# Grouped attention in smaller units: one pair of heads and 512 queries at a time, in a two-block transformer kernel

## The chip, the core and the metric

The kernel runs on one core of one Trainium2 chip. The metric is the time of the whole program on the device in microseconds (us), from its first to its last instruction with what little lies around them. Before the change the median of 3 runs is 2143.96 us (2143.17 to 2151.37).

Five engines work beside each other, each with a queue of its own that it takes strictly in order: TensorE (PE: matmuls, and PEld for loading the weights of one), VectorE (DVE), ScalarE (ACT), GpSimd (POOL) and SyncE (SP, which here only starts transfers). They meet at semaphores alone: an instruction may wait until a semaphore has reached a number, and may raise one when it ends.

## The reference

The program is two blocks with an attention and a feed-forward part each. The change touches one of the four parts only, the attention with grouped heads ahead of the first mixture of experts, over T = 2048 tokens of width 128:

```
N_HEADS = 16;  N_KV = 4;  NUM_REP = 4;  HEAD_DIM = 8
q = (x @ qw + qb).reshape(B, S, N_HEADS, HEAD_DIM).transpose(0, 2, 1, 3)
k = (x @ kw + kb).reshape(B, S, N_KV, HEAD_DIM).transpose(0, 2, 1, 3)      # v alike
k = jnp.repeat(k, NUM_REP, axis=1)
scores = jnp.einsum('bhqd,bhkd->bhqk', q, k) / np.sqrt(HEAD_DIM).astype(np.float32)
attn = jax.nn.softmax(scores, axis=-1)
out = jnp.einsum('bhqk,bhkd->bhqd', attn, v)
out = out.transpose(0, 2, 1, 3).reshape(B, S, D)
return out @ ow + ob
```

Four query heads share each of the four key heads. Every head has 2048 x 2048 scores, and all of them are made, exponentiated, and multiplied by the values.

## The kernel before

The attention is cut into NU = 16 units. A unit is one key head (with its four query heads, two pairs of two) and 512 queries (one of NC = 4 chunks). For every unit the kernel does two things.

**Maxima.** The softmax subtracts each row's maximum. To have it, the scores are made once in the layout of queries by keys (`pe_job`, L847: two matmuls of a pair of heads, 128 queries by 512 keys each, into two banks of PSUM), and VectorE reduces both banks at once (`v_job`, L865, 128x1024). There are UM = 32 such jobs in a unit. After the last of them VectorE folds the partial maxima (MM, L871), GpSimd negates them and splits them in three bf16 parts (`g_neg`), TensorE turns them into rows (job "rows", L850), VectorE copies these out (NMP, L875), and SP writes them by 12 small transfers into three extra rows of the queries' operand QST (`sp_gqa_rows`, L907), so that the next kind of matmul subtracts the maximum by itself.

**Scores, exponentials, values.** For each of the 16 tiles of 128 keys (kt) and each of the two pairs (jj) there is a step, 32 in a unit. I call the step's number i = 2 kt + jj. TensorE makes the scores of the pair again, now keys by queries (`pe_gqa`, L942: two matmuls of 512 columns into two of the three banks 0 to 2, which go round). ScalarE takes the exponential of each bank (`act_gqa`, L986) and writes it to the probability buffer PB (a part of `tmpb`), which holds two key tiles of four heads. TensorE then multiplies values by probabilities (`pe_values`, L920), in half queries: step i multiplies the half jj of the key tile before for all four heads, four matmuls on 32 columns of the array each, accumulating in bank 3. After the unit's last key tile both halves are still due and follow in one go.

**The end of a unit.** ScalarE copies bank 3 to PV (`act_values`, L974) after the first key tile of the next unit, TensorE turns PV (job "values", L854, in step i = 3 of the next unit), and VectorE divides by the sums (L881 a reciprocal, L883 a multiplication).

The order of the work is written out by hand. `ahead(u, i)` says which jobs TensorE and VectorE do in step i of unit u: always one maximum job, EARLY = 12 steps ahead of where it belongs; "rows" four steps after the last maximum of a unit; "values" in step 3. `first_jobs` lists what is done ahead of the first step: the 32 maxima of unit 0, three of unit 1, rows of unit 0, and nine more of unit 1, 44 maxima in all. Jobs take turns on two sets of two banks (4 and 5, 6 and 7), so TensorE can begin job n when VectorE has finished job n-2 (`s_mfree`).

The waits that matter, each with its semaphore: a step's score matmuls wait for the first of the two exponentials of the step before (`s_exp`, since three banks go round); an exponential waits for its scores (`s_qk`), the first one of a key tile also for the values of two key tiles before (`s_pv`, since PB holds two); the values of a key tile wait for its last exponential (`s_exp`), those of a new unit also for the copy of bank 3 (`s_pvc`). The first step waits for the rows (`s_row`) and for the stacked queries and keys (`s_stack_rest`: transfers through `scr_q` and `scr_k`, started by `sp_stacks` and `act_stacks`).

Of the kernel before, what the change touches and what calls it, by code (L numbers as in the profile page):

```python
# [16 lines left out]
F32 = mybir.dt.float32  # L17
# [6 lines left out]
P = 128  # L24
T = 2048
# [32 lines left out]
def build(nc, A, out):  # L58

    ctx = ExitStack()  # L60
    with ctx:
# [62 lines left out]
        def cs(c):  # L124
            return slice(CH * c, CH * c + CH)
# [548 lines left out]
        PAIRS = H0 // 2  # L674
        NU = NKV * NC
        QST = sb("QST", [P, PAIRS, T], BF16, b0)
        KST = sb("KST", [P, NKV, T], BF16, b0)
# [7 lines left out]
        MX = sb("MX", [P, 2, 2, TPC, NC], F32, b0)  # L685
        MM = sb("MM", [P, 2 * 2 * TPC], F32, b0)
        NG = sb("NG", [P, 2 * 2 * TPC], F32, b0)
        NB3 = sb("NB3", [P, 3, 2 * 2 * TPC], BF16, b0)
        NMP = sb("NMP", [3 * 2 * 2 * TPC, 2, P], BF16, b0)
        identb = sb("identb", [P, P], BF16, b0)  # L690
        RD = sb("RD", [P, TPC, REP], F32, b0)
        scr_q = nc.dram_tensor("scr_q", (3, P, T), BF16).ap()
# [11 lines left out]
        s_const2 = sem("s_const2")  # L704
        UI = NT * REP
        UM = UI // 2
        EARLY, LATE = 12, 3

        def ahead(u, i):

            jobs = []
            if i == 3 and u:
                jobs.append(("values", u - 1))
            v, m = u + 1 + (i + EARLY) // UM, (i + EARLY) % UM
            if v < NU:
                jobs.append(("max", v, m))
            if i + EARLY == UM + LATE and u + 1 < NU:
                jobs.append(("rows", u + 1))
            return jobs

        first_jobs = [("max", 0, m) for m in range(UM)] + [("max", 1, m) for m in range(LATE)] + [("rows", 0)] + \
                     [("max", 1, m) for m in range(LATE, EARLY)]
        job_at = {job: n for n, job in enumerate(first_jobs + [j for u in range(NU) for i in range(UM) for j in ahead(u, i)]
                                                 + [("values", NU - 1)])}

# [108 lines left out]
        def pe_job(pe, job):  # L834
            n, what, u = job_at[job], job[0], job[1]
            b = mbank(n)
            if what == "rows":
                pe.wait_ge(s_neg, u + 1)
            if what == "values":
                pe.wait_ge(s_pvc, u + 1)  # L840
            if n >= 2:
                pe.wait_ge(s_mfree, n - 1)
            if what == "max":
                g, qc, (jj, t, kc) = u // NC, u % NC, (job[2] // (TPC * NC), job[2] // NC % TPC, job[2] % NC)
                for x in range(2):
                    r = slice(64 * x, 64 * x + SK)
                    pe.matmul(PS[:, b + x, :], QST[r, 2 * g + jj, CH * qc + P * t:CH * qc + P * t + P], KST[r, g, cs(kc)],  # L847
                              start=True, stop=True).then_inc(s_mjob, 1)
            elif what == "rows":
                pe.matmul(PS[0:3 * 2 * 2 * TPC, b, 0:P], NB3[:, :, :].rearrange("p a m -> p (a m)"), identb[:, :],  # L850
                          start=True, stop=True).then_inc(s_mjob, 2)
            else:
                for t in range(TPC):
                    m = pe.transpose(PS[:, b, P * t:P * t + P], PV[:, P * t:P * t + P], ident[:, :])  # L854
                m.then_inc(s_mjob, 2)

        def v_job(v, chain, job):
# [3 lines left out]
            if what == "max":  # L861
                m = job[2]
                if m == 0 and u:
                    v.wait_ge(s_mm, u)
                r = v.tensor_reduce(MX[:, :, m // (TPC * NC), m // NC % TPC, m % NC], PS[:, b:b + 2, :], AX.X, ALU.max)  # L865
                if m < UM - 1:
                    r.then_inc(s_mfree, 1)
                else:
                    chain.link(r)
                    v.sem_inc(s_mfree, 1)  # L870
                    v.tensor_reduce(MM[:, :], MX[:, :, :, :, :].rearrange("p x j t k -> p (x j t) k"), AX.X, ALU.max).then_inc(s_mm, 1)  # L871
            elif what == "rows":
                if u >= 2:
                    v.wait_ge(s_row[u % 2], ROWS * (u // 2))
                v.tensor_copy(NMP[:, u % 2, :], PS[0:3 * 2 * 2 * TPC, b, 0:P]).then_inc(s_nmp, 1)  # L875
                v.wait_ge(s_nmp, u + 1)
                v.sem_inc(s_mfree, 1)
            else:
                g, qc = u // NC, u % NC
                b7 = PS[:, b, :].rearrange("p (t j c) -> p t j c", t=TPC, j=REP)  # L880
                chain.link(v.reciprocal(RD[:, :, :], b7[:, :, :, HD]))  # L881
                ao = AO[:, TPC * qc:TPC * qc + TPC, 32 * g:32 * g + 32].rearrange("p t (j c) -> p t j c", j=REP)
                v.tensor_tensor(ao, b7[:, :, :, 0:HD], RD[:, :, :].unsqueeze(3).to_broadcast([P, TPC, REP, HD]), ALU.mult).then_inc(s_ao, 1)  # L883
# [15 lines left out]
        def sp_gqa_rows(sp):  # L899
            for u in range(NU):  # L900
                g, qc = u // NC, u % NC
                sp.wait_ge(s_nmp, u + 1)
                for a in range(3):
                    for x in range(2):
                        for jj in range(2):
                            at = 2 * 2 * TPC * a + 2 * TPC * x + TPC * jj
                            sp.dma_start(QST[64 * x + SK + a:64 * x + SK + a + 1, 2 * g + jj, cs(qc)].rearrange("r (t p) -> r t p", p=P),  # L907
                                         NMP[at:at + TPC, u % 2, :]).then_inc(s_row[u % 2], 16)

        ROWS = 3 * 2 * 2 * 16  # L910

        def pe_values(pe, u, kt, half):

            if half == 0:
                if kt == 0 and u:
                    pe.wait_ge(s_pvc, u)
                pe.wait_ge(s_exp, u * UI + (kt + 1) * REP)
            h = slice(CH // 2 * half, CH // 2 * (half + 1))
            for j in range(REP):
                last = pe.matmul(PS[32 * j:32 * j + 32, 3, h], VS[:, kt, u // NC, :], PB[:, kt % 2, j, h],  # L920
                                 start=(kt == 0 and half == 0), stop=(kt == NT - 1 and half == 1),
                                 tile_position=(0, 32 * j), skip_group_check=True)
            if half:
                last.then_inc(s_pv, 1)

        def pe_gqa(pe):
# [4 lines left out]
            pe.wait_ge(s_stack_rest, STACKED)  # L931
            for u in range(NU):
                g, qc = u // NC, u % NC
                pe.wait_ge(s_row[u % 2], ROWS * (u // 2 + 1))
                for i in range(UM):
                    kt, jj = i // 2, i % 2
                    at = UI * u + 2 * i
                    if at >= 2:
                        pe.wait_ge(s_exp, at - 1)
                    for x in range(2):  # L940
                        r = slice(64 * x, 64 * x + SR)
                        pe.matmul(PS[:, (at + x) % 3, :], KST[r, g, P * kt:P * kt + P], QST[r, 2 * g + jj, cs(qc)],  # L942
                                  start=True, stop=True).then_inc(s_qk, 1)
                    for job in ahead(u, i):
# [24 lines left out]
        def act_values(a, u):  # L969

            a.wait_ge(s_pv, NT * (u + 1))
            if u:
# [3 lines left out]
        def act_gqa(a):  # L976
            for u in range(NU):
                for kt in range(NT):
                    if kt == 1 and u:
                        act_values(a, u - 1)  # L980
                    if NT * u + kt >= 2:
                        a.wait_ge(s_pv, NT * u + kt - 1)
                    for j in range(REP):
                        at = UI * u + REP * kt + j
                        a.wait_ge(s_qk, at + 1)
                        a.activation(PB[:, kt % 2, j, :], PS[:, at % 3, :], ACT.Exp, scale=HD ** -0.5).then_inc(s_exp, 1)  # L986
            act_values(a, NU - 1)
# [4 lines left out]
        def v_gqa(v, chain):  # L992
            for job in first_jobs:
                v_job(v, chain, job)
            for u in range(NU):
                for i in range(UM):
                    for job in ahead(u, i):
                        v_job(v, chain, job)
# [1013 lines left out]
```

## Time and profile before

| | us |
|---|---|
| median of 3 runs | 2143.96 |
| the profiled execution | 2147.42 |
| its span, first to last instruction | 2145.6 |
| reductions for maxima, VectorE, L865 x512 | 585.3 busy, 1217 ns each |
| exponentials, ScalarE, L986 x1024 | 554.0 busy, 595 ns each |
| values, TensorE, L920 x4096 | 326.4 busy, 393 ns each |
| scores for the exponentials, TensorE, L942 x1024 | 201.4 busy, 390 ns each |
| scores for the maxima, TensorE, L847 x1024 | 206.6 busy, 401 ns each |
| VectorE, share of the whole span | 64% |
| TensorE, share of the whole span | 80% |

Consecutive instructions overlap inside an engine, so a busy time is not a rate: what one instruction costs in a row of equals is the distance of their starts. In the rows further down, an entry with "xN" is N instructions merged, its duration reaches from the first one's start to the last one's end, and an idle time in brackets stands in front of an entry where the engine had nothing to do, with the one that ended it. A matmul in fp32 is shown as two instructions. The first score matmul for an exponential starts at 466.14 us, the last values are multiplied at 1107.16 us; that stretch is what the change is about.

### The profile page before, as it was taken

Reading aid. Unit: us, or ns where it says so; the run is one execution under the profiler, and the core shown is the slowest. Engines: PE = TensorE matmul, PEld = TensorE weight load, DVE = VectorE, ACT = ScalarE, POOL = GpSimd, SP = SyncE. Lnnn points to the kernel's source line nnn. Section 1 sums busy time; section 2 is a strip of 40 time slices with the busy share of each in tenths; the row PEclk is TensorE's granted clock in tenths of the full one; section 3 lists DMA queues with packets and bytes.
Section 4 is the critical chain, followed back from the end, with each engine's and each line's share of the span. In section 5 each row is a group of like instructions: output and inputs, shape, how many; then the busy total and the mean of one; then the engine's idle time right before and its main releaser. Section 6 shows DMA issues by size and latency. Waiting matters only on the chain.

```text
span 2145.6 us, 27944 instructions
## 1 busy us (share of the span) xinstructions
PE 1723.7 (80%) x10324; PEld 786.0 (37%) x10324; DVE 1363.8 (64%) x2683; ACT 1163.1 (54%) x2116; POOL 267.3 (12%) x336
## 2 busy tenths in 40 slices
PE   3599237269999999999875994989899988489998
PEld 2599225012222222222223442444444444334443
DVE  3898775599999999999622335556656656322222
ACT  3465103028888888888862336556666655212222
POOL 1265003000000000000000002111111111111110
PEclk7899658559999999999996996999999999699999
DMA  1000000430000000000012420000000000122320
GB/s 40 1 1 1 0 0 8 93 47 2 2 2 2 2 2 2 2 2 2 17 26 41 84 63 1 4 12 16 15 15 15 15 0 1 30 43 47 59 51 29
DMA packets 76094, 42.58 MB, mean 20 GB/s; under 512 B 21920, under 2 KB 72224, under 8 KB 75840
## 3 DMA queue, kind: packets, MB, share of 16 engines
q1 hardware_dynamic: 74576, 37.90, 8.6%
q10 hardware_dynamic: 1392, 3.02, 0.7%
q8 instruction: 77, 1.26, 0.3%
q14 instruction: 49, 0.40, 0.1%
HBM read 37.55 MB, written 3.15 MB: 19 GB/s over the span
## 4 chain that ended last, share of the span: by engine, by line
PE 52%; DVE 30%; ACT 7%; DMA 4%; issue 4%; POOL 1%; SPq 0%; ACTq 0%; DVEq 0%; POOLq 0%
DVE MX L865 17%; PE PS L1347 6%; PE PS L920 5%; PE PS L1353 5%; PE PS L1779 4%; PE PS L1780 4%; PE PS L1789 4%; PE PS L942 3%; DMA SB<-scr_w 3%; PE PS L433 3%; PE PS L1298 3%; ACT tmpb L986 3%; PE PS L1317 2%; PE PS L1189 2%; DVE MS L534 2%
## 5 line engine op out<-in xcount | busy, mean ns | idle before, releaser
L986 ACT ACTIVATE tmpb<-PS 128x512 f32<-128x512 f32 x1024 | 554.0, 595 | 143.0 <-PE PS L942 126.5
L865 DVE TENSOR_REDUCE MX<-PS 128x2 f32<-128x1024 f32 x512 | 585.3, 1217 | 52.7 <-PE PS L847 48.9
L920 PE MATMUL PS<-tmpb,VS 128*32 128x256 f32 x4096 | 326.4, 393 | 14.0 <-ACT tmpb L986 6.6
L847 PE MATMUL PS<-KST,QST 56*128 56x512 bf16 x1024 | 206.6, 401 | 61.6 <-DMA KST<-scr_k 34.3
L942 PE MATMUL PS<-QST,KST 59*128 59x512 bf16 x1024 | 201.4, 390 | 21.2 <-ACT tmpb L986 17.0
L1814 DVE TENSOR_TENSOR HG<-HG,PS 128x512 f32<-128x512 f32 (+1 forms) x96 | 65.9, 686 | 199.3 <-PE PS L1780 199.3
L1804 ACT ACTIVATE HG<-PS 128x512 f32<-128x512 f32 (+1 forms) x96 | 57.2, 595 | 207.7 <-PE PS L1779 207.7
L920 PEld LDWEIGHTS PS<-tmpb,VS 128*32 128x32 f32 x4096 | 82.5, 108 | 179.0 <-issue 85.0
L942 PEld LDWEIGHTS PS<-QST,KST 59*128 59x128 bf16 x1024 | 49.2, 93 | 244.3 <-ACT tmpb L986 229.8
L1347 PE MATMUL PS<-X,WF 128*128 128x512 f32 x256 | 128.4, 636 | 4.2 <-ACT X L1492 4.2
L1508 ACT ACTIVATE HF<-PS,CL 128x512 f32<-128x512 f32 x128 | 87.9, 687 | 68.7 <-PE PS L1347 68.7
L1353 PE MATMUL PS<-HF,WF 128*128 128x512 f32 x256 | 116.4, 592 | 0.0
L1779 PE MATMUL PS<-XS,G 128*128 128x512 f32 (+1 forms) x192 | 99.3, 598 | 11.6 <-POOLq L1753 11.6
L1605 DVE TENSOR_SCALAR N<-PS,BA,RR 128x128 f32<-128x128 f32 x256 | 86.0, 404 | 25.7 <-POOL RR L1651 14.4
L1780 PE MATMUL PS<-XS,G 128*128 128x512 f32 (+1 forms) x192 | 98.9, 597 | 0.0
L1632 DVE TENSOR_TENSOR Y<-G2B,X 128x512 f32<-128x512 f32 x32 | 22.1, 692 | 119.1 <-ACT G2B L1516 119.1
L1789 PE MATMUL PS<-HG,G 128*128 128x512 f32 (+1 forms) x192 | 96.8, 592 | 0.0
L1212 DVE TENSOR_TENSOR HID<-HID,SB 128x512 f32<-128x512 f32 x64 | 42.6, 690 | 82.2 <-DMA SB<-scr_w 43.8
L433 PE MATMUL PS<-BIG,ident 128*128 128x128 f32 x512 | 66.6, 285 | 30.2 <-DVE BIG L370 30.2
L1298 PE MATMUL PS<-HT,WA 128*128 128x512 f32 x192 | 90.8, 606 | 0.1
L847 PEld LDWEIGHTS PS<-KST,QST 56*128 56x128 bf16 x1024 | 50.1, 95 | 110.8 <-DVE MX L865 54.5
L166 PE MATMUL PS<-ident,XN 128*128 128x128 f32 x80 | 21.7, 426 | 84.7 <-ACT XN L155 69.9
(293 smaller groups left out, 2491.5 us busy)
## 6 DMA issues: line engine op xcount, KB each, us to landing
SB<-scr_w SPq DMA_DIRECT2D x16, 1024.0 KB, 14.4
WF<-in_L_attn_Wf SPq DMA_DIRECT2D x16, 256.0 KB, 3.0
QST<-NMP SPq DMA_DIRECT2D x192, 1.0 KB
G<-in_L_ffn_w SPq DMA_DIRECT2D x16, 176.0 KB, 2.4
QST<-scr_q SPq DMA_DIRECT2D x14, 192.0 KB
W<-in_L_ffn_w SPq DMA_DIRECT2D x16, 128.0 KB, 2.1
scr_q<-tmpb SPq DMA_DIRECT2D x3, 512.0 KB, 2.7
KST<-scr_k ACTq DMA_DIRECT2D x14, 96.0 KB
```

The lines of the kernel that those rows point to most:

```text
L433: pe.matmul(PS[:, x, 0:HH * SCOL], ident[:, :], PR[:, i, heads(x), :].rearrange("p h c -> p (h c)"), start=i == 0, stop=False, skip_group_ ...
L847: pe.matmul(PS[:, b + x, :], QST[r, 2 * g + jj, CH * qc + P * t:CH * qc + P * t + P], KST[r, g, cs(kc)], start=True, stop=True).then_inc(s ...
L865: r = v.tensor_reduce(MX[:, :, m // (TPC * NC), m // NC % TPC, m % NC], PS[:, b:b + 2, :], AX.X, ALU.max)
L920: last = pe.matmul(PS[32 * j:32 * j + 32, 3, h], VS[:, kt, u // NC, :], PB[:, kt % 2, j, h], start=(kt == 0 and half == 0), stop=(kt == NT ...
L942: pe.matmul(PS[:, (at + x) % 3, :], KST[r, g, P * kt:P * kt + P], QST[r, 2 * g + jj, cs(qc)], start=True, stop=True).then_inc(s_qk, 1)
L986: a.activation(PB[:, kt % 2, j, :], PS[:, at % 3, :], ACT.Exp, scale=HD ** -0.5).then_inc(s_exp, 1)
L1298: pe.matmul(PS[:, bank, :], WA[:, b % 2, j, :], HT[:, cs(c)], start=True, stop=True).then_inc(done, 1)
L1347: pe.matmul(PS[:, 3 + j % 2, :], WF1[:, b % 2, P * j:P * j + P], X1[:, n % 2, :], start=True, stop=True).then_inc(s_f1, 1)
L1353: f = pe.matmul(PS[:, 5, :], WF2[:, b % 2, j, :], HF[:, j, :], start=(j == 0), stop=(j == KF - 1))
L1779: pe.matmul(PS[0:w, b, :], G1[:, k, f:f + w], XS[:, c % 2, :], start=True, stop=True).then_inc(s_h, 1)
L1780: last = pe.matmul(PS[0:w, b + 1, :], G3[:, k, f:f + w], XS[:, c % 2, :], start=True, stop=True)
L1789: pe.matmul(PS[:, c, :], G2[0:w, k, m, :], HG[0:w, o % 4, :], start=False, stop=False, skip_group_check=True).then_inc(s_hfree, 1)
```

## The change

A unit of the steps is now one pair of heads and 512 queries, so a unit has 16 steps (one for each key tile) and there are NV = 2 x NU = 32 of them, s = 0 to 31; even s is the first pair of a key head and a chunk, odd s the second. Maxima, their fold, their negation and their rows are made for each of the 32, with half as many numbers each; the rows take 6 transfers in place of 12. A step multiplies the values of both heads of the pair and both halves of the queries of the key tile before (again four matmuls on 32 columns of the array). PB holds four key tiles of two heads in the same memory, and the exponentials of a step wait for the values of four steps before. Bank 3 is still copied, turned and divided once for two units (after the odd one), with the columns in another order, for which VectorE needs two reciprocals and two multiplications. EARLY and LATE stay 12 and 3, so that 28 maxima lie ahead of the first step.

```diff
-        PB = tmpb[:, 0:4 * T].bitcast(F32).rearrange("p (b j n) -> p b j n", b=2, j=REP)
+        PB = tmpb[:, 0:4 * T].bitcast(F32).rearrange("p (b x n) -> p b x n", b=4, x=2)
-        UI = NT * REP
-        UM = UI // 2
+        UM = NT
         EARLY, LATE = 12, 3
...
-            if i == 3 and u:
-                jobs.append(("values", u - 1))
-            v, m = u + 1 + (i + EARLY) // UM, (i + EARLY) % UM
-            if v < NU:
+            if i == 3 and s % 2 == 0 and s:
+                jobs.append(("values", s // 2 - 1))
+            v, m = s + 1 + (i + EARLY) // UM, (i + EARLY) % UM
+            if v < NV:
                 jobs.append(("max", v, m))
-            if i + EARLY == UM + LATE and u + 1 < NU:
-                jobs.append(("rows", u + 1))
+            if i + EARLY == UM + LATE and s + 1 < NV:
+                jobs.append(("rows", s + 1))
...
-                b7 = PS[:, b, :].rearrange("p (t j c) -> p t j c", t=TPC, j=REP)
-                chain.link(v.reciprocal(RD[:, :, :], b7[:, :, :, HD]))
...
+                for h in range(2):
+                    last = v.reciprocal(RD[:, h, :, :, :], b7[:, :, :, :, h, HD])
+                chain.link(last)
+                for h in range(2):
...
+                    last = v.tensor_tensor(ao, b7[:, :, :, :, h, 0:HD], RD[:, h, :, :, :].unsqueeze(4).to_broadcast([P, 2, 2, 2, HD]), ALU.mult)
+                last.then_inc(s_ao, 1)
...
-        def pe_values(pe, u, kt, half):
-
-            if half == 0:
-                if kt == 0 and u:
-                    pe.wait_ge(s_pvc, u)
-                pe.wait_ge(s_exp, u * UI + (kt + 1) * REP)
...
+        def pe_values(pe, s, kt):
+
+            g, qc, jj = where(s)
+            n = NT * s + kt
+            if kt == 0 and jj == 0 and s:
+                pe.wait_ge(s_pvc, s // 2)
+            pe.wait_ge(s_exp, 2 * (n + 1))
+            for x in range(2):
+                for h in range(2):
...
-            for u in range(NU):
-                g, qc = u // NC, u % NC
-                pe.wait_ge(s_row[u % 2], ROWS * (u // 2 + 1))
-                for i in range(UM):
-                    kt, jj = i // 2, i % 2
-                    at = UI * u + 2 * i
+            for s in range(NV):
+                g, qc, jj = where(s)
+                pe.wait_ge(s_row[s % 2], ROWS * (s // 2 + 1))
+                for kt in range(NT):
+                    at = 2 * (NT * s + kt)
...
                     if kt:
-                        pe_values(pe, u, kt - 1, jj)
-                pe_values(pe, u, NT - 1, 0)
-                pe_values(pe, u, NT - 1, 1)
+                        pe_values(pe, s, kt - 1)
+                pe_values(pe, s, NT - 1)
...
-                    if NT * u + kt >= 2:
-                        a.wait_ge(s_pv, NT * u + kt - 1)
-                    for j in range(REP):
+                    n = NT * s + kt
+                    if n >= 4:
+                        a.wait_ge(s_pv, n - 3)
+                    for x in range(2):
```

On VectorE, in the middle of the attention, one whole unit of before stands in this order (MX a reduction for maxima, MM their fold, NMP the rows' copy, RD and tmpb the division):

```order
L881 RECIPROCAL RD<-PS 128x16 [waits s_mjob]
L883 TENSOR_TENSOR tmpb<-PS,RD 128x4x32 [waits ch_v]
L865 TENSOR_REDUCE MX<-PS 128x2 [waits s_ao,s_mjob]
L865 TENSOR_REDUCE MX<-PS 128x2 [waits s_mjob] x16
L871 TENSOR_REDUCE MM<-MX 128x16 [waits ch_v]
L865 TENSOR_REDUCE MX<-PS 128x2 [waits s_mm,s_mjob]
L865 TENSOR_REDUCE MX<-PS 128x2 [waits s_mjob] x3
L875 CAST NMP<-PS 48x128 [waits s_row0,s_mjob]
L865 TENSOR_REDUCE MX<-PS 128x2 [waits s_nmp,s_mjob]
L865 TENSOR_REDUCE MX<-PS 128x2 [waits s_mjob] x10
```

Of now, from the second instruction of a division to past the second fold:

```order
L886 RECIPROCAL RD<-PS 128x8
L890 TENSOR_TENSOR tmpb<-PS,RD 128x2x2x16 [waits ch_v]
L890 TENSOR_TENSOR tmpb<-PS,RD 128x2x2x16
L869 TENSOR_REDUCE MX<-PS 128x2 [waits s_ao,s_mjob]
L875 TENSOR_REDUCE MM<-MX 128x8 [waits ch_v]
L869 TENSOR_REDUCE MX<-PS 128x2 [waits s_mm,s_mjob]
L869 TENSOR_REDUCE MX<-PS 128x2 [waits s_mjob] x3
L879 CAST NMP<-PS 24x128 [waits s_row1,s_mjob]
L869 TENSOR_REDUCE MX<-PS 128x2 [waits s_nmp,s_mjob]
L869 TENSOR_REDUCE MX<-PS 128x2 [waits s_mjob] x11
L875 TENSOR_REDUCE MM<-MX 128x8 [waits ch_v]
L869 TENSOR_REDUCE MX<-PS 128x2 [waits s_mm,s_mjob]
```

Fold and rows' copy come after 16 reductions where they came after 32, the first fold now right behind the division; the division has two more instructions.

On TensorE, this is the seam between two units before, from the last values of the old one to the first values of the new one (L942 scores for the exponentials, L847 scores for the maxima, L920 values):

```order
L920 MATMUL PS<-tmpb,VS 32x256 [waits s_exp]
L920 MATMUL PS<-tmpb,VS 32x256 x7
L942 MATMUL PS<-QST,KST 128x512 [waits s_exp,s_row0]
L942 MATMUL PS<-QST,KST 128x512
L847 MATMUL PS<-KST,QST 128x512 [waits s_mfree]
L847 MATMUL PS<-KST,QST 128x512
L942 MATMUL PS<-QST,KST 128x512 [waits s_exp]
L942 MATMUL PS<-QST,KST 128x512
```

Now, with L949, L851 and L929 in their places:

```order
L929 MATMUL PS<-tmpb,VS 32x256 [waits s_exp]
L929 MATMUL PS<-tmpb,VS 32x256 x3
L949 MATMUL PS<-QST,KST 128x512 [waits s_exp,s_row0]
L949 MATMUL PS<-QST,KST 128x512
L851 MATMUL PS<-KST,QST 128x512 [waits s_mfree]
L851 MATMUL PS<-KST,QST 128x512
L949 MATMUL PS<-QST,KST 128x512 [waits s_exp]
L949 MATMUL PS<-QST,KST 128x512
L851 MATMUL PS<-KST,QST 128x512 [waits s_mfree]
L851 MATMUL PS<-KST,QST 128x512
L929 MATMUL PS<-tmpb,VS 32x256 [waits s_exp,s_pvc]
```

Such a seam stands between two units; there are 31 where there were 15. Four of the values' matmuls are left for it where there were eight, and the first values of the new unit come one step sooner.

## Rows read from the trace of the kernel before

**Rows 1.** Timeline of VectorE, one whole unit: start, us, engine, line, what [idle].
```profile
793.97 19.32 DVE L865 TENSOR_REDUCE MX<-PS 128x2 f32<-128x1024 f32 x17 [0.15 <-DVE tmpb L883]
813.44 0.22 DVE L871 TENSOR_REDUCE MM<-MX 128x16 f32<-128x64 f32 x1 [0.15 <-DVE MX L865]
813.77 4.62 DVE L865 TENSOR_REDUCE MX<-PS 128x2 f32<-128x1024 f32 x4
818.31 0.27 DVE L875 CAST NMP<-PS 48x128 bf16<-48x128 f32 x1
818.91 9.14 DVE L865 TENSOR_REDUCE MX<-PS 128x2 f32<-128x1024 f32 x8 [0.33 <-PE PS L847]
829.32 3.49 DVE L865 TENSOR_REDUCE MX<-PS 128x2 f32<-128x1024 f32 x3 [1.26 <-PE PS L847]
833.41 0.26 DVE L881 RECIPROCAL RD<-PS 128x16 f32<-128x16 f32 x1 [0.61 <-PE PS L854]
834.15 2.36 DVE L865 TENSOR_REDUCE MX<-PS 128x2 f32<-128x1024 f32 x2 [0.15 <-DVE tmpb L883]
```
**Rows 2.** Timeline of TensorE, the seam between two units.
```profile
826.08 0.39 PE L942 MATMUL PS<-QST,KST 59*128 59x512 bf16 x2
...
827.64 1.07 PE L920 MATMUL PS<-tmpb,VS 128*32 128x256 f32 x16 [0.39 <-ACT tmpb L986]
828.64 0.39 PE L942 MATMUL PS<-QST,KST 59*128 59x512 bf16 x2
...
829.77 0.39 PE L942 MATMUL PS<-QST,KST 59*128 59x512 bf16 x2 [0.53 <-ACT tmpb L986]
...
831.83 0.64 PE L920 MATMUL PS<-tmpb,VS 128*32 128x256 f32 x8 [0.37 <-ACT PV L974]
832.40 0.39 PE L942 MATMUL PS<-QST,KST 59*128 59x512 bf16 x2
```
**Rows 3.** Timeline of TensorE, two steps in the middle of a unit (8 and 9).
```profile
798.51 0.39 PE L942 MATMUL PS<-QST,KST 59*128 59x512 bf16 x2
...
799.65 0.39 PE L942 MATMUL PS<-QST,KST 59*128 59x512 bf16 x2
...
800.75 0.39 PE L942 MATMUL PS<-QST,KST 59*128 59x512 bf16 x2
```
**Rows 4.** Timeline of ScalarE, the first exponential of each of these two steps.
```profile
798.99 0.60 ACT L986 ACTIVATE tmpb<-PS 128x512 f32<-128x512 f32 x1
...
800.07 0.60 ACT L986 ACTIVATE tmpb<-PS 128x512 f32<-128x512 f32 x1
```
**Rows 5.** Timeline of TensorE, two steps of the last unit, which has no maxima.
```profile
1082.08 0.39 PE L942 MATMUL PS<-QST,KST 59*128 59x512 bf16 x2
...
1083.21 0.39 PE L942 MATMUL PS<-QST,KST 59*128 59x512 bf16 x2
...
1084.29 0.39 PE L942 MATMUL PS<-QST,KST 59*128 59x512 bf16 x2
```
**Rows 6.** Who waited for the values' matmuls (L920): us, times.
```profile
  ACT PV L974: 1.2, 1
```
**Rows 7.** Timeline of SP and TensorE at the start of the steps.
```profile
454.89 7.50 SPq L907 DMA_DIRECT2D QST<-NMP  x12
466.14 0.61 PE L942 MATMUL PS<-QST,KST 59*128 59x512 bf16 x2 [2.06 <-DMA QST<-NMP]
```
**Rows 8.** Busy time by stretch: from:to, length, engines, PEclk, DMA share, GB/s.
```profile
460.00:462.00 2.00, 1.22 (x4) 0.21 (x4) 2.00 (x3) 0.00 (x0) 0.00 (x0) 0.50 0.50 59
462.00:464.00 2.00, 1.14 (x4) 0.21 (x4) 2.00 (x3) 0.00 (x0) 0.00 (x0) 0.50 0.09 5
826.00:834.00 8.00, 6.25 (x68) 1.95 (x64) 6.09 (x7) 6.30 (x13) 0.00 (x0) 1.00 0.00 0
1071.00:1077.00 6.00, 5.98 (x38) 1.84 (x42) 0.55 (x2) 3.29 (x7) 0.00 (x0) 0.50 0.24 36
```
**Rows 9.** Groups of VectorE by form: a small operation of another stage.
```profile
L137 DVE TENSOR_TENSOR vh<-vh,ag 128x4 f32<-128x4 f32 x8 | 1.4, 179 | 0.3
```

More of the change, by code:

```diff
@@ L675, in build @@
         NU = NKV * NC
+        NV = 2 * NU
         QST = sb("QST", [P, PAIRS, T], BF16, b0)
@@ L843, in pe_job @@
             if what == "max":
-                g, qc, (jj, t, kc) = u // NC, u % NC, (job[2] // (TPC * NC), job[2] // NC % TPC, job[2] % NC)
+                (g, qc, jj), (t, kc) = where(u), (job[2] // NC, job[2] % NC)
                 for x in range(2):
@@ L887, in g_neg @@
         def g_neg(g, chain):
-            for u in range(NU):
+            for u in range(NV):
                 g.wait_ge(s_mm, u + 1)
@@ L899, in sp_gqa_rows @@
         def sp_gqa_rows(sp):
-            for u in range(NU):
-                g, qc = u // NC, u % NC
-                sp.wait_ge(s_nmp, u + 1)
+            for s in range(NV):
+                g, qc, jj = where(s)
+                sp.wait_ge(s_nmp, s + 1)
                 for a in range(3):
                     for x in range(2):
[L905 to L910, printed above, removed]
-        def pe_values(pe, u, kt, half):
-            if half == 0:
-                if kt == 0 and u:
-                    pe.wait_ge(s_pvc, u)
-                pe.wait_ge(s_exp, u * UI + (kt + 1) * REP)
-            h = slice(CH // 2 * half, CH // 2 * (half + 1))
-            for j in range(REP):
[L920 to L924, printed above, removed]
+                        at = 2 * TPC * a + TPC * x
+                        sp.dma_start(QST[64 * x + SK + a:64 * x + SK + a + 1, 2 * g + jj, cs(qc)].rearrange("r (t p) -> r t p", p=P),
+                                     NMP[at:at + TPC, s % 2, :]).then_inc(s_row[s % 2], 16)
+        ROWS = 3 * 2 * 16
+        def pe_values(pe, s, kt):
[6 more added lines that the diff above has]
+                for h in range(2):
+                    r = 32 * (2 * x + h)
+                    last = pe.matmul(PS[r:r + 32, 3, CH // 2 * jj:CH // 2 * (jj + 1)], VS[:, kt, g, :],
+                                     PB[:, n % 4, x, CH // 2 * h:CH // 2 * (h + 1)], start=kt == 0, stop=kt == NT - 1,
+                                     tile_position=(0, r), skip_group_check=True)
+            last.then_inc(s_pv, 1)
         def pe_gqa(pe):
@@ L931, in pe_gqa @@
             pe.wait_ge(s_stack_rest, STACKED)
[L932 to L937 removed]
+            for s in range(NV):
+                g, qc, jj = where(s)
+                pe.wait_ge(s_row[s % 2], ROWS * (s // 2 + 1))
+                for kt in range(NT):
+                    at = 2 * (NT * s + kt)
                     if at >= 2:
@@ L943, in pe_gqa @@
                                   start=True, stop=True).then_inc(s_qk, 1)
-                    for job in ahead(u, i):
+                    for job in ahead(s, kt):
                         pe_job(pe, job)
                     if kt:
-                        pe_values(pe, u, kt - 1, jj)
-                pe_values(pe, u, NT - 1, 0)
-                pe_values(pe, u, NT - 1, 1)
+                        pe_values(pe, s, kt - 1)
+                pe_values(pe, s, NT - 1)
             pe_job(pe, ("values", NU - 1))
@@ L994, in v_gqa @@
                 v_job(v, chain, job)
-            for u in range(NU):
+            for s in range(NV):
                 for i in range(UM):
-                    for job in ahead(u, i):
+                    for job in ahead(s, i):
                         v_job(v, chain, job)
```

44 lines of the change are left out of this document (22 added, 22 removed).

## The prediction

> **What bounds the kernel now.** I first split the span by stage. The steps of this attention run from 466.14 us [rows 7] to the last values at 1107.16 us, some 641 us; the rest of the program is not touched. VectorE, ScalarE and TensorE are all busy nearly nine tenths of that stretch, so shares of busy time decide nothing, and I went to the timeline of one unit on VectorE. From the reduction that starts at 793.97 to its like at 834.15 a unit takes 40.18 us [rows 1]. Inside an unbroken row the reductions start 1.132 us apart ((9.14 - 1.217)/7, with 1217 ns for one), and 32 of them make 36.22 us. The other 3.97 us are four interruptions, each read as the distance of two reductions less 1.132:
> - the fold MM: 813.77 less 812.08, the start of the last of the 17: 0.56;
> - the rows' copy NMP: 818.91 less 817.17: 0.61, of which 0.33 is idle until TensorE is past the job that it shares a pair of banks with;
> - the seam between units: 829.32 less 826.83: 1.36, nearly all idle, with TensorE's maxima late;
> - bank 3's copy and the division: 834.15 less 831.58: 1.44.
> 36.22 + 3.97 = 40.19, so VectorE's queue tells the whole unit, and the reader is to see that it has no idle time but at these places.
>
> TensorE is a hair faster. Two steps in mid-unit take 1.14 and 1.10 us [rows 3], 1.12 on average, so that it gains 0.01 a step on VectorE and then waits for a pair of banks. It has a limit of its own: scores, exponential, scores. In the even step the exponential begins 0.48 after its scores begin (798.51 to 798.99), lasts 0.60, and 0.06 later the next scores start; in the odd one it begins after 0.42 [rows 3, 4]. Only the even step's first exponential has a second wait, that for PB. In the last unit, with no maxima at all, the steps are still 1.13 and 1.08 [rows 5]. So three things lie within 3%: VectorE's 1.132, the round of three banks at 1.14 or 1.08, and TensorE's own work. What PB's size allows is none of them: the values' matmuls are waited for once, for 1.2 us, by bank 3's copy and never by an exponential [rows 6].
>
> The seam explains itself on TensorE [rows 2]. The last scores of the unit start at 826.08; the values of the last key tile need the exponential of these very scores and start at 827.64, 1.56 later; 16 instructions (both halves) run until the next unit's scores at 828.64. That is 2.56 where a step takes 1.13, so 1.43 lost, of which 1.36 reach VectorE.
>
> **The change part by part.** All terms count from the profiled execution's 2147.42 us (span 2145.6); the median of the runs is 3.46 lower, and I carry the differences over to it.
>
> *Buffers.* Four of two heads in the same bytes. As no exponential waits for the old ones [rows 6], this gives nothing: 0. The wait moves from every second step to every step, so that all steps may take the 1.14 of the even ones [rows 3, 4]. VectorE's 1.132 hides nearly all; uncovered it would be 484 steps x 0.008 = 4 us, which I keep for the upper end.
>
> *Fold and rows.* The same reductions (512) in 32 groups. One more fold (0.56) and one more rows' copy (0.61) for each of 16 old units, each with half the numbers; but of 0.22 and 0.27 us for the instructions themselves little depends on the size, and the rest is waiting. Ends: 0.4 and 0.5 each if size counts, 0.56 and 0.61 if not; I take the latter. 16 x 0.56 = 9.0 and 16 x 0.61 = 9.8. GpSimd and SP have twice the calls at half the length. SP took 7.50 us to start 12 transfers [rows 7], so 6 take 3.8; the rows are copied nine steps ahead of their use, over 9 us, and are not waited for.
>
> *Seams.* 31 in place of 15. A new one is shorter, since only one step's values (8 instructions) are left: these took 0.57 from start to the next scores at 831.83 to 832.40, while 16 took 1.00 [rows 2]. The wait for the exponential stays 1.56, since it belongs to the last scores whatever the unit. So 1.56 + 0.57 = 2.13, less 1.13 is 1.00, less the 0.07 of lead that TensorE has gathered: 0.93. The step after it is held by the round of banks at 1.13 (828.64 to 829.77 [rows 2]), as now, and the next already carries values. Before: 14 x 1.36 and the last one, where no maxima follow, at the full 1.43, 20.5 in all. After: 30 x 0.93 and one at 1.0, 28.9. Difference 8.4. Its ends: 0.8 and 1.05 a seam, so 4.3 to 12.
>
> *Division.* As often as before, with the same wait for bank 3's copy (831.83 [rows 2]), but with two instructions more on VectorE. Each costs from 0.18, a tiny operation [rows 9], to 0.26, the whole reciprocal now [rows 1]; they have half the elements, so I take 0.20, 0.4 for both, times 16: 6.4. Right behind it come the last reduction of a unit and its fold, so that TensorE must wait for banks there; but VectorE works through, so nothing more is added.
>
> *The head.* 28 maxima ahead of the first step in place of 44, 16 x 1.132 = 18.1 us less on VectorE. But the first step also waits for the stacked queries and keys. The transfers run at a share of 0.50 of the queues until 462 and at 0.09 in the next two us [rows 8], and the 12 small rows' transfers, started from 454.89 on, lie behind them in SP's queue and let TensorE go at 466.14 [rows 7]. With 6 of them, that end comes about 1.1 us earlier (half of the two or three us after the large ones). So -1.1 of the 18.1; the ends are 0 and -3. The 16 maxima are then made beside 16 of the last steps, which slow from 1.105 to 1.132: +0.4.
>
> *The tail.* After the last exponential 8 instructions in place of 16: -0.4. In the old last unit the clock was down at 0.50 for about 6 us after its seam [rows 8], which cost some 2 us; the new last seam has one idle step less, and I take half of it: -1.0, ends 0 and -2.
>
> Sum: 9.0 + 9.8 + 8.4 + 6.4 - 1.1 + 0.4 - 0.4 - 1.0 = +31.5 us. Against 2143.96 that is 2175.5, I say 2175 (a profiled execution of about 2179). With all terms at their low ends (6.4 + 8.0 + 4.3 + 5.8 - 3 + 0.4 - 0.4 - 2 = 19.5) it is 2163, with the high ones (9.0 + 9.8 + 12 + 8.3 + 0 + 0.4 - 0.4 + 0 + 4 = 43) 2187.
>
> **The rivals.**
>
> *A. VectorE's doubled small work is hidden.* Folds, rows' copies and the longer division would fall into time in which VectorE sits idle anyway; of the sum 25.2 go and 6.3 stay: 2150, which a measurement can't tell from no change. This decides if TensorE, not VectorE, sets the pace: 25.2/16 = 1.6 us more per 32 steps must fit in, so its steps would have to be over 1.132 + 1.6/32 = 1.18 us. For it: each step now has the slower exponential. Against: steps are 1.14 at most [rows 3], and VectorE's row of 17 reductions has no gap [rows 1].
>
> *B. The head gives all of its 18.1 us.* Then it is 17 less, 2158. For it: TensorE's last wait is for the rows [rows 7], which would come 18 us sooner. Against: the large transfers still run at 462 [rows 8], and the first step needs them.
>
> *C. The clock falls at the seams.* After the seam without maxima the granted clock was 0.50, the 1.2 GHz level, for 6 us; through one with maxima it is 1.00, the 2.4 GHz level [rows 8]. If the 31 seams each brought it down at some 2 us, it would be 2175 + 62 = 2237. Against: a new seam has less idle time (0.39, then about 0.5 in one step, and in every second unit 0.4 for bank 3's copy) than the old one, whose 0.39, 0.53 and 0.37 [rows 2] did not. The Trainium skill, in TensorE: Matmul & The Clock Gate (section on the HAM clock gate), says that the gate follows how busy TensorE has been of late and halves the clock after idling; by that rule, the trace's last seam agrees, and shorter but more frequent idling could go either way.
>
> *D. The four buffers let ScalarE run ahead and the seams vanish.* Minus 28.9, so 2147. For it: the copy's position. Against: the values stand ahead of the next scores in TensorE's queue, and [rows 6].
>
> **How the numbers follow.** Forecast 0.81, A 0.06, B 0.04, C 0.04, D 0.05. The forecast's own ends are 2163 and 2187; I widen it down to B, 2158 to 2188, with nearly a tenth of the forecast itself outside. About 0.5% (11 us) is what can be told from no change: above 2155 lie the forecast, B and C, 0.89 with a little of the forecast's tail given away; within 2133 to 2155 A and D, 0.08; below it 0.03, for A or D coming together with a gain at the head.
>
> **What would show it.** Right: on VectorE two seams of about 0.9, two folds and two rows' copies in each stretch of 32 reductions, which takes 42.2 us (40.2 now); TensorE's scores 2.13 apart at a seam; the first step at about 465.0 with VectorE idle some 17 us ahead of it; the last values about 30 us later than at 1107. Wrong: a first step near 448; idle time of VectorE inside a unit; a granted clock under 1.00 between 480 and 1060; exponentials that start without a gap over a seam.

## The result: 1.4% slower, and the profile after

The changed kernel takes 2179.72 us (median of 6 runs, 2175.44 to 2187.18), beside 2149.02 for the kernel before (6 runs, 2143.17 to 2152.26). The ratio is 1.0144, 95% interval 1.0119 to 1.0169: slower by 31 us, where +31.5 was forecast.

The profiled execution after took 2176.03 us (span 2174.3, so 28.7 more than the one before). The timeline of VectorE over one stretch of two new units, from division to division, answers to [rows 1] (start, us, engine, line, what; L869 a reduction, L875 the fold, L879 the rows' copy, L886 and L890 the division):

```profile
846.04 0.28 DVE L886 RECIPROCAL RD<-PS 128x8 f32<-128x8 f32 x2 [0.25 <-PE PS L858]
...
853.68 9.15 DVE L869 TENSOR_REDUCE MX<-PS 128x2 f32<-128x1024 f32 x8 [0.33 <-PE PS L851]
863.79 4.63 DVE L869 TENSOR_REDUCE MX<-PS 128x2 f32<-128x1024 f32 x4 [0.97 <-PE PS L851]
868.58 0.19 DVE L875 TENSOR_REDUCE MM<-MX 128x8 f32<-128x32 f32 x1 [0.15 <-DVE MX L869]
868.87 4.62 DVE L869 TENSOR_REDUCE MX<-PS 128x2 f32<-128x1024 f32 x4
873.41 0.27 DVE L879 CAST NMP<-PS 24x128 bf16<-24x128 f32 x1
874.00 9.15 DVE L869 TENSOR_REDUCE MX<-PS 128x2 f32<-128x1024 f32 x8 [0.33 <-PE PS L851]
884.12 2.36 DVE L869 TENSOR_REDUCE MX<-PS 128x2 f32<-128x1024 f32 x2 [0.97 <-PE PS L851]
886.80 1.23 DVE L869 TENSOR_REDUCE MX<-PS 128x2 f32<-128x1024 f32 x1 [0.32 <-PE PS L851]
888.28 0.28 DVE L886 RECIPROCAL RD<-PS 128x8 f32<-128x8 f32 x2 [0.25 <-PE PS L858]
888.59 0.35 DVE L890 TENSOR_TENSOR tmpb<-PS,RD 128x64 f32<-128x64 f32 x2
889.10 1.23 DVE L869 TENSOR_REDUCE MX<-PS 128x2 f32<-128x1024 f32 x1 [0.15 <-DVE tmpb L890]
890.48 0.19 DVE L875 TENSOR_REDUCE MM<-MX 128x8 f32<-128x32 f32 x1 [0.15 <-DVE MX L869]
890.78 4.62 DVE L869 TENSOR_REDUCE MX<-PS 128x2 f32<-128x1024 f32 x4
895.31 0.27 DVE L879 CAST NMP<-PS 24x128 bf16<-24x128 f32 x1
895.91 9.15 DVE L869 TENSOR_REDUCE MX<-PS 128x2 f32<-128x1024 f32 x8 [0.33 <-PE PS L851]
```

From 853.68 to its like at 895.91 it is 42.23 us, where 42.2 was forecast and 40.18 stood before [rows 1]. The reader is to see two seams (0.97 idle each), two folds and two rows' copies. Taken as before, as distances less 1.132 (the first seam: 863.79 less 861.61, the start of the last of the eight, less 1.13), they are: seams 1.05 and 1.06, folds 0.54 and 0.55, rows' copies 0.60 and 0.60, bank 3's copy with the division 0.41 + 1.17 = 1.58; 36.22 + 5.98 = 42.20.

On TensorE, the seam that answers to [rows 2] and two steps in mid-unit that answer to [rows 3]:

```profile
813.01 0.39 PE L949 MATMUL PS<-QST,KST 59*128 59x512 bf16 x2
...
814.15 0.39 PE L949 MATMUL PS<-QST,KST 59*128 59x512 bf16 x2
...
815.28 0.39 PE L949 MATMUL PS<-QST,KST 59*128 59x512 bf16 x2
...
818.69 0.39 PE L949 MATMUL PS<-QST,KST 59*128 59x512 bf16 x2
...
820.31 0.64 PE L929 MATMUL PS<-tmpb,VS 128*32 128x256 f32 x8 [0.44 <-ACT tmpb L992]
820.88 0.39 PE L949 MATMUL PS<-QST,KST 59*128 59x512 bf16 x2
...
822.02 0.39 PE L949 MATMUL PS<-QST,KST 59*128 59x512 bf16 x2 [0.53 <-ACT tmpb L992]
```

The first exponentials of the steps at 813.01 and 814.15, which answer to [rows 4] (timeline of ScalarE):

```profile
813.49 0.60 ACT L992 ACTIVATE tmpb<-PS 128x512 f32<-128x512 f32 x1
...
814.63 0.60 ACT L992 ACTIVATE tmpb<-PS 128x512 f32<-128x512 f32 x1
```

Both begin 0.48 after their scores; the 0.42 of every second step is gone. The two steps are 1.14 and 1.13, not 1.14 and 1.10. The seam is 820.88 - 818.69 = 2.19, of which the wait for the exponential is 1.62 (1.56 before) and the half set of values 0.57.

The ends of the stretch, that answer to [rows 7, 8] (timeline of TensorE; then busy time of the stretch 1110 to 1140, in which the last seam lies, with PEclk ahead of the two columns of transfers):

```profile
461.00 0.61 PE L949 MATMUL PS<-QST,KST 59*128 59x512 bf16 x2 [15.07 <-DMA QST<-NMP]
...
1133.57 0.64 PE L929 MATMUL PS<-tmpb,VS 128*32 128x256 f32 x8 [0.50 <-ACT tmpb L992]
```
```profile
1110.00:1140.00 30.00, 24.62 (x238) 8.49 (x231) 0.80 (x5) 24.28 (x45) 0.00 (x0) 1.00 0.24 52
```

The steps last 672.6 us, 31.6 more than the 641.0 of before; without its head the sum had 32.6. The first step comes 5.1 us sooner than at 466.14, and the last values 26.4 later. Behind the last values 2.2 us are added, which the sum didn't have. They come from a stage that the change doesn't touch and that waits for transfers: two stations of the chain of waits there, the router and a late turn in its stage, are 148.0 us apart in the profile of before (1138.14 and 1286.11) and 151.6 after, while the parts ahead of and behind these two are together 1.4 us shorter than before:

```profile
1164.20 6.98 PE PS L1036 x32
...
1315.83 1.10 PE PS L1231 x4
```

31.6 - 5.1 + 2.2 = 28.7, the difference of the spans.

### The profile page after: what moved, and what is told of

Its sections match the earlier page's. It is cut to its first block, busy times and chain, and to the rows that moved or that the text cites. A ratio compares the mean times of both kernels' runs of the same rounds, so it can differ in the third digit from the quotient of the medians.

```text
span 2174.3 us, 28502 instructions
## 1 busy us (share of the span) xinstructions
PE 1728.7 (80%) x10340; PEld 774.1 (36%) x10340; DVE 1376.6 (63%) x2747; ACT 1165.4 (54%) x2116; POOL 286.0 (13%) x432
## 4 chain that ended last, share of the span: by engine, by line
PE 57%; DVE 24%; ACT 8%; DMA 5%; issue 5%; POOL 1%; SPq 0%; ACTq 0%; DVEq 0%; POOLq 0%
DVE MX L869 11%; PE PS L929 8%; PE PS L1353 6%; PE PS L1359 5%; PE PS L949 5%; PE PS L1785 4%; PE PS L1786 4%; PE PS L1795 4%; DMA SB<-scr_w 3%; ACT tmpb L992 3%; PE PS L433 3%; PE PS L1304 3%; PE PS L851 3%; PE PS L1323 2%; PE PS L1195 2%
## 5 line engine op out<-in xcount | busy, mean ns | idle before, releaser
L869 DVE TENSOR_REDUCE MX<-PS 128x2 f32<-128x1024 f32 x512 | 591.6, 1219 | 86.7 <-PE PS L851 81.1
L929 PE MATMUL PS<-tmpb,VS 128*32 128x256 f32 x4096 | 327.6, 391 | 22.2 <-ACT tmpb L992 14.3
L851 PE MATMUL PS<-KST,QST 56*128 56x512 bf16 x1024 | 202.7, 393 | 54.0 <-DMA KST<-scr_k 32.4
L949 PE MATMUL PS<-QST,KST 59*128 59x512 bf16 x1024 | 200.3, 388 | 32.6 <-ACT tmpb L992 17.2
L929 PEld LDWEIGHTS PS<-tmpb,VS 128*32 128x32 f32 x4096 | 80.8, 108 | 209.5 <-ACT tmpb L992 180.0
L949 PEld LDWEIGHTS PS<-QST,KST 59*128 59x128 bf16 x1024 | 49.1, 93 | 256.3 <-ACT tmpb L992 228.0
L901 POOL TENSOR_SCALAR NG<-MM 128x8 f32<-128x8 f32 x32 | 7.5, 233 | 680.3 <-DVE MM L875 680.3
```

The lines of the kernel that those rows point to most:

```text
L869: r = v.tensor_reduce(MX[:, :, m // NC, m % NC], PS[:, b:b + 2, :], AX.X, ALU.max)
L929: last = pe.matmul(PS[r:r + 32, 3, CH // 2 * jj:CH // 2 * (jj + 1)], VS[:, kt, g, :], PB[:, n % 4, x, CH // 2 * h:CH // 2 * (h + 1)], star ...
```

## The experiments

The time of a run is uneven by some 10 us, and in the profiles the first step alone comes up to 15 us apart (below). So two readings stand beside each other: the ratio to the kernel before on the same chip, and the **period**, the time on VectorE from one division to the next in the middle of the attention. It repeats to 0.01 us in most stretches of a profile. Up to five of the fifteen (none before, two in the change) are longer, by at most 0.5 us, for a cause that stays open, and the last one or two, where the maxima run out, are shorter. It is 40.18 before and 42.23 after.

| run | what | ratio to before, 95% interval | median, before beside it | period |
|---|---|---|---|---|
| the change | | 1.0144 [1.0119, 1.0169] | 2179.72, 2149.02 | 42.23 |
| e1 | new steps, old maxima | 1.0042 [1.0023, 1.0060] | 2159.05, 2151.83 | 40.67 |
| e2 | old steps, new maxima | 1.0080 [1.0058, 1.0103] | 2168.66, 2151.83 | 41.29 |
| e3 | the change without seams | 1.0005 [0.9986, 1.0024] | 2152.87, 2151.83 | 40.27 |
| e4 | before without seams | 0.9896 [0.9872, 0.9921] | 2128.93, 2151.83 | 38.76 |
| e5 | the change, half the division | 1.0108 [1.0081, 1.0135] | 2174.57, 2148.78 | 42.02 |
| e6 | the change, two buffers | 1.0186 [1.0169, 1.0203] | 2187.35, 2148.78 | 42.23 |
| e7 | the change, a wait every second step | 1.0138 [1.0106, 1.0171] | 2178.92, 2148.78 | 41.95 |
| e8 | e4, division behind the maximum | 0.9869 [0.9850, 0.9888] | 2121.78, 2148.78 | 38.42 |
| e9 | e8, rows ahead of the maximum | 0.9847 [0.9822, 0.9872] | 2120.14, 2153.06 | 38.43 |
| e10 | new steps, no seams, as e8 | 0.9861 [0.9833, 0.9890] | 2123.19, 2153.06 | 38.66 |

The expectations of e5 to e7 give the changed kernel's period as 42.11. That was taken from a division's second reciprocal to the next one's first; from first to first, as in this table, it is 42.23.

**e1 and e2: each half of the change alone.** In e1 the steps are the changed kernel's and the jobs those of before:

```diff
-                    for job in ahead(s, kt):
+                    for job in ahead(s // 2, NT * jj + kt):
```

Expected: 

> The new steps (units of a pair, values as two heads by two halves, four buffers) with the maxima as they were before the change: folds and rows once for 32 reductions, 12 transfers, 44 maxima ahead of the first step. Theory (the terms add up on VectorE's queue): the 18.8 us of folds and rows' copies go, the seams (+8.4), the division (+6.4) and the small gains at the tail (-1.4) stay: 13 us over before, some 2162. Rival (TensorE's steps, each with the slower exponential, set the pace and cover VectorE's small work): nothing goes, 31 over before, 2180.

Measured: 9 us over before by the ratio (5 to 13), not 31: the rival is out. Its period is 0.49 over before, where the terms gave 0.9 (0.5 for the seams, 0.4 for the division). Both terms are smaller. The division with bank 3's copy costs 1.57, only 0.13 over the 1.44 of before. And one of the two seams on the timeline of VectorE, the one that follows the division, costs 0.61, so that both together, at 1.66, are 0.3 over the one seam of before.

```profile
791.28 14.80 DVE L871 TENSOR_REDUCE MX<-PS 128x2 f32<-128x1024 f32 x13 [0.15 <-DVE tmpb L892]
806.61 4.63 DVE L871 TENSOR_REDUCE MX<-PS 128x2 f32<-128x1024 f32 x4 [0.53 <-PE PS L853]
...
816.86 9.15 DVE L871 TENSOR_REDUCE MX<-PS 128x2 f32<-128x1024 f32 x8 [0.33 <-PE PS L853]
826.97 2.36 DVE L871 TENSOR_REDUCE MX<-PS 128x2 f32<-128x1024 f32 x2 [0.97 <-PE PS L853]
```

The seam at 806.61 has 0.53 of idle time, that at 826.97 has 0.97. I read this so: after the division VectorE is behind TensorE and works that off in the first seam; where a rows' copy lies between, as always in the changed kernel, VectorE has already waited 0.33 for TensorE there and starts the seam with nothing in hand. No run varied this by itself.

In e2 the steps are those of before, and each pair has its own fold and rows:

```diff
-            v, m = u + 1 + (i + EARLY) // UM, (i + EARLY) % UM
+            v, m = divmod(2 * UM * u + i + 44, UM)
...
-            if i + EARLY == UM + LATE and u + 1 < NU:
-                jobs.append(("rows", u + 1))
+            if m == LATE and v - 1 < NV:
+                jobs.append(("rows", v - 1))
```

Expected: 

> The old steps (units of two pairs, old values, old buffers, old division) with the maxima folded, negated and written as rows for each pair, still 44 ahead of the first step. Theory: 16 more folds at 0.56 and 16 more rows' copies at 0.61, 18.8 us over before, some 2168. Rival (this small work falls into idle time): within 3 us of before.

Measured: 17 us (12 to 22), period + 1.11 where 0.56 + 0.61 = 1.17 was said. The doubled small work counts in full. The second fold and the second rows' copy, on the timeline of VectorE, with the reduction behind each:

```profile
829.55 0.19 DVE L876 TENSOR_REDUCE MM<-MX 128x8 f32<-128x32 f32 x1 [0.15 <-DVE MX L870]
829.85 4.62 DVE L870 TENSOR_REDUCE MX<-PS 128x2 f32<-128x1024 f32 x4
834.38 0.27 DVE L880 CAST NMP<-PS 24x128 bf16<-24x128 f32 x1
834.98 9.14 DVE L870 TENSOR_REDUCE MX<-PS 128x2 f32<-128x1024 f32 x8 [0.33 <-PE PS L852]
```

**e3 and e4: the seams away.** The values of a unit's last key tile are multiplied in the next unit's first step (in e4, its first two), behind its scores:

```diff
-                    if kt:
-                        pe_values(pe, s, kt - 1)
-                pe_values(pe, s, NT - 1)
+                    n = NT * s + kt
+                    if n:
+                        pe_values(pe, (n - 1) // NT, (n - 1) % NT)
+            pe_values(pe, NV - 1, NT - 1)
```

Expected: 

> The changed kernel with the values of a unit's last key tile multiplied in the first step of the next unit, behind its scores, so that no seam is left in TensorE's queue. Theory (31 seams cost 0.93 us each on VectorE): 26 to 29 us less than the changed kernel, 2151 to 2154. Rival (the seams' idle time is a reserve that the folds and rows' copies use up anyway, and the wait for bank 3's copy grows in its place): 5 to 10 less, 2170 to 2175.

> The kernel before with the values of a unit's last key tile multiplied in the first two steps of the next unit. Theory (15 seams at 1.36 us): 18 to 20 us less than before, 2129 to 2131; it needs no new buffers. Rival (bank 3's copy now comes a step later, TensorE waits for it in the third step, and ScalarE is behind): at most 8 less, 2141 or more.

Measured: e3 has 1.0005 where the change has 1.0144, 30 us less; its period is 1.96 shorter, for two seams. e4 is 22 us under before (17 to 28), its period 1.42 shorter for one seam. Both gain a little more than was expected, and both rivals are out. The timeline of VectorE in e4 has no idle time left in the place of the seam:

```profile
811.19 4.62 DVE L865 TENSOR_REDUCE MX<-PS 128x2 f32<-128x1024 f32 x4
815.73 0.27 DVE L875 CAST NMP<-PS 48x128 bf16<-48x128 f32 x1
816.32 12.53 DVE L865 TENSOR_REDUCE MX<-PS 128x2 f32<-128x1024 f32 x11 [0.32 <-PE PS L847]
829.41 0.26 DVE L881 RECIPROCAL RD<-PS 128x16 f32<-128x16 f32 x1 [0.56 <-PE PS L854]
```

**e5: half the division.** Both loops over `h` run once; half of the attention's outputs are neither divided nor written.

Expected: 

> The changed kernel with one reciprocal and one multiplication of each division instead of two (half of the outputs are not divided and not written). Theory (VectorE's queue is the bound, each small instruction counts in full): the period of two units on VectorE, 42.11 us in the changed kernel, falls by the distances of two small instructions, 0.3 to 0.45, so 5 to 7 us in all. Rival (they hide behind TensorE's four turns of bank 3 and the maximum job): the period stays within 0.05.

Measured: the period falls by 0.21, less than said, and the ratio by 0.4% with intervals that overlap. The timeline of VectorE in e5 has the reason; the changed kernel's two reciprocals take 0.28 together and its two multiplications 0.35:

```profile
815.72 0.21 DVE L886 RECIPROCAL RD<-PS 128x8 f32<-128x8 f32 x1 [0.25 <-PE PS L858]
815.96 0.23 DVE L890 TENSOR_TENSOR tmpb<-PS,RD 128x64 f32<-128x64 f32 x1
```

So a second small instruction behind its like lengthens the pair by 0.07 and 0.12 us, not by its duration.

**e6: two buffers in place of four.**

```diff
-                    if n >= 4:
-                        a.wait_ge(s_pv, n - 3)
+                    if n >= 2:
+                        a.wait_ge(s_pv, n - 1)
```

with `n % 2` for `n % 4` in both uses of PB.

Expected: 

> The changed kernel with two probability buffers of two heads in place of four (a step's exponentials wait for the values of two steps before). Theory (TensorE does these values ahead of the scores that the exponential waits for, so the buffer is never what is late): period 42.11 us, within 0.05. Rival (the four buffers carry ScalarE over the seams and over bank 3's copy, where it would else wait): the period grows by 0.3 or more at the two seams, 5 us or more in all.

Measured: the same 42.23, to the hundredth. The ratio is 1.0186, 0.4% over the change's with intervals that just touch. Of the 7.9 us between the two profiled executions 5.9 lie ahead of the first step, which came at 466.92, and 1.6 in the steps, where four stretches have a longer period and in the change's profile two; whether the buffers have a part in these 1.6 us, one profile of each can't tell. The seams and the copy of bank 3 are as in the change, so the rival's 0.3 or more is out: in the period four buffers give nothing over two.

**e7: the wait that was thought hidden.**

```diff
-                    if n >= 4:
-                        a.wait_ge(s_pv, n - 3)
+                    if n >= 4 and n % 2 == 0:
+                        a.wait_ge(s_pv, n - 2)
```

Expected: 

> The changed kernel, but ScalarE asks for the values only at every second step, then for those of two steps at once. Theory (the second wait before an exponential delays it by 0.06 us although what it asks for is long done): steps in mid-unit alternate between 1.14 and 1.10 us again, TensorE gains 0.07 of lead by a seam, and the period falls from 42.11 by 0.1 to 0.2, 2 to 3 us in all. Rival (the odd and even steps differ by something else, such as the wait of the values): all steps stay at 1.14 and the period at 42.11.

Measured: the period falls by 0.28, a bit more than expected. The steps of TensorE alternate again:

```profile
817.65 0.39 PE L949 MATMUL PS<-QST,KST 59*128 59x512 bf16 x2
...
818.76 0.39 PE L949 MATMUL PS<-QST,KST 59*128 59x512 bf16 x2
...
819.89 0.39 PE L949 MATMUL PS<-QST,KST 59*128 59x512 bf16 x2
...
821.00 0.39 PE L949 MATMUL PS<-QST,KST 59*128 59x512 bf16 x2
```

1.11, 1.13 and 1.11, with the first exponential 0.42 and 0.48 behind its scores by turns. The idle time at a seam, on VectorE, is 0.84 in place of 0.97:

```profile
814.97 9.14 DVE L869 TENSOR_REDUCE MX<-PS 128x2 f32<-128x1024 f32 x8 [0.33 <-PE PS L851]
824.95 4.62 DVE L869 TENSOR_REDUCE MX<-PS 128x2 f32<-128x1024 f32 x4 [0.84 <-PE PS L851]
```

As a distance less 1.132 this seam costs 0.92, and on TensorE 2.13 from scores to scores: these are the prediction's 0.93 and 2.13. By the period the wait is worth 16 x 0.28 = 4.5 us; from first step to last values the two profiles differ by 3.3, since some stretches of e7 are longer. The ratio, 1.0138, can't tell so little.

**e8 and e9: a better version.** e8 is e4 with the "values" job behind the maximum in its step; e9 also has "rows" ahead of the maximum in its step.

```diff
-            if i == 3 and u:
-                jobs.append(("values", u - 1))
...
                 jobs.append(("rows", u + 1))
+            if i == 3 and u:
+                jobs.append(("values", u - 1))
```

Expected: 

> The kernel before with values carried over the seam (e4), and in the fourth step of a unit the maximum job ahead of the turn of bank 3 rather than behind it. Theory (VectorE idles 0.56 us before each division, while TensorE turns bank 3 with no maximum waiting; with the maximum made first it reduces in that time): period 38.76 less 0.3 to 0.56, 2120 to 2125. Rival (the idle time moves to the next maximum, which TensorE makes 0.6 us later): period and time as in e4, 2129.

> e8 with, in the step that has the rows job, this job ahead of the maximum instead of behind it. Theory (VectorE idles 0.33 us after the rows' copy because the next maximum is made behind this step's values and the next step's scores; with a maximum right behind the rows that is filled): period 38.42 less 0.2 to 0.33, 2117 to 2119. Rival (TensorE then waits for the bank pair of the maximum instead, and nothing is gained): 38.42 within 0.05, 2122.

Measured: e8 shortens e4's period by 0.34 and is 28 us under before (24 to 32); e9 adds nothing to the period. In e9's timeline (VectorE, and TensorE's next maximum) the 0.33 of idle time stands behind the rows' copy as ever. TensorE can't have the next maximum ready: its banks are those of the reduction ahead of the copy, which ends at 803.66, and TensorE starts 0.06 later. So the expectation had the reason wrong, and the prediction, which put these 0.33 on the shared banks, had it right.

```profile
800.17 3.49 DVE L865 TENSOR_REDUCE MX<-PS 128x2 f32<-128x1024 f32 x3
...
803.57 0.27 DVE L875 CAST NMP<-PS 48x128 bf16<-48x128 f32 x1
...
803.72 0.39 PE L847 MATMUL PS<-KST,QST 56*128 56x512 bf16 x2 [0.81 <-DVE MX L865]
...
804.17 13.67 DVE L865 TENSOR_REDUCE MX<-PS 128x2 f32<-128x1024 f32 x12 [0.33 <-PE PS L847]
818.06 1.23 DVE L865 TENSOR_REDUCE MX<-PS 128x2 f32<-128x1024 f32 x1 [0.23 <-PE PS L847]
```

**e10: the new steps under the best of conditions.** e1 with the seams away, the jobs in e8's order and e7's wait.

Expected: 

> The new steps (units of a pair, four buffers, longer division, ScalarE asking for the values at every second step) with the old maxima, the values carried over the seam and the division behind the maximum as in e8. It asks whether the new steps are worth anything once seams and folds are out of the way. Theory (VectorE's 1.132 us a reduction is the bound, buffers give nothing): period 38.42 plus 0.05 to 0.2, 2122 to 2126. Rival (four buffers pay once the seams are gone): period under 38.3, 2118 or less.

Measured: 38.66, 0.24 over e8, a little more than the 0.2 expected and near the 0.21 that the two small instructions cost in e5. With seams and folds out of the way, the new steps are still no gain.

## Why the prediction was right, point by point

- **VectorE's queue as the measure of a unit.** Right. Every period above is 36.22 us of reductions and the interruptions between them; e1 and e2 both moved by interruptions alone. That the terms simply add is shown but for one place: e1, whose first seam cost 0.61 and not 0.93.
- **Fold and rows, 18.8 us.** Right: 0.55 and 0.60 each after; 1.11 a period in e2, 16 x 1.11 = 17.8 us.
- **Seams, 8.4 us.** The mechanism was right and the size too small. A new seam costs 1.06 and not 0.93, 31 of them 32.9, so 12.4 more than the 20.5 of before. Two causes: TensorE has no lead to spend any more (0.07), and the wait for the exponential is 0.06 longer. Both come from the step called "Buffers": with the second wait at every second step only, the seam of e7 costs 0.92.
- **Buffers, 0 and at most 4 us.** Half right. The buffers themselves give nothing to the period (e6). But that the wait at every step is hidden by VectorE's 1.132 was wrong: VectorE covers the steps in between, and the lead that TensorE no longer gathers is missing at the next seam, where the longer wait stands open too. e7 puts both at 0.28 a period, 4.5 us in all by the period and 3.3 by the profiles, which the sum had only at its upper end. These are the same microseconds as the 4.0 that the seams' term lacks.
- **Division, 6.4 us.** Too large. The two more instructions cost 0.19 on VectorE and 0.21 of the period (e5), 3.4 us; bank 3's copy and the division went from 1.44 to 1.58, 2.2 us.
- So the total of the steps was right partly by luck: seams (4.0 too little) and division (4.2 too much) went against each other, and each of the two lies beyond the ends that the prediction gave it (4.3 to 12 us, and 5.8 to 8.3).
- **Head, -1.1 us.** Not shown. The profile of the change has its first step 5.1 us sooner, at 461.00 and not at 465.0, but no run speaks for a part of the change in it: where the maxima go by pairs (28 of them ahead of the first step, in e2 44) the first step came at 461.00, 472.51, 471.38, 474.25, 466.92 and 465.47 us (the change, e2, e3, e5, e6, e7), where they go by two pairs at 466.14, 459.63, 474.14, 470.94, 466.29 and 469.22 (before, e1, e4, e8, e9, e10). That the large transfers hold it, so that rival B's 18 us don't come, is right: TensorE stood idle 15.07 us there, and the share of the transfers was still 0.42 from 450 to 460 and 0.00 in the next two us, in which the first step starts.
- **Tail, -1.0 us for the clock.** A bit more. The last seams now pass at a granted clock of 1.00, and the six steps behind the one with bank 3's copy, from scores to scores, take 7.9 us where they took 9.8. So about all of the 2 us is gone.
- **The rivals.** A fell with e2, B with the head, D with the 0.97 of idle time at every seam and with e6. C fell with the profile: the clock stayed at 1.00, the 2.4 GHz level, through the seams (below, the busy time of the stretch 480 to 1060 after). That fits the Trainium skill's TensorE: Matmul & The Clock Gate (section on the HAM clock gate), by which the clock follows how busy TensorE is; no run here varied that alone.

```profile
480.00:1060.00 580.00, 518.55 (x5359) 134.48 (x5351) 525.80 (x551) 482.03 (x893) 32.91 (x164) 1.00 0.01 2
```

## What to carry to other kernels

Where two engines run within a few per cent of each other, count per round what interrupts the fuller queue: halving the unit doubled every fold, copy and seam, and that was most of the loss; the second wait at every step was a good part of the rest. Look at the seam between units in the queue of the engine that both wait for; moving the last product behind the next unit's scores (e4) took away the seam that the change doubled, and with the division moved as well (e8) the kernel is 1.3% faster than before (1.0 to 1.5), with its old buffers and units. A buffer is worth adding only where some row shows a wait for it.

## What the runs showed of the hardware that was not expected

- A second wait on an instruction costs about 0.06 us even when what it asks for is long done: the exponential with two waits begins 0.48 us after its scores begin and that with one 0.42 [rows 3, 4]; with two waits at every step all steps have 0.48 (the change), and taking the second wait from every other step gives those steps their 0.42 back (e7).
- A small VectorE instruction behind an independent one of its kind adds 0.07 us (reciprocal) or 0.12 us (multiplication), though one alone lasts 0.21 or 0.23 us (e5).
- The transfers at the head land unevenly, by more than most of the effects above. In the twelve profiles, one of each kernel, the first maximum, which waits for such a transfer, starts on VectorE between 410.2 and 420.2 us, and the first step between 459.6 and 474.3; the period is blind to it.
